# Token statistics summed in the state space, and an MLP that walks row block by row block

## The chip, the cores and the metric

The kernel runs on one core of one Trainium2 chip. The metric is the device time of one execution in microseconds; for the kernel before it is the median of three runs. The engines are named as in the profile: PE (TensorE), DVE (VectorE), ACT (ScalarE), POOL (GpSimd) and SP, which here only issues DMAs.

## The reference

Two transformer layers on 2048 tokens of width 512, batch 1, float32. Layer 0 is an attention and a mixture of eight experts; layer 1 is a selective state space and a block-diagonal MLP on permuted features. The change touches the last two parts:

```python
h = _layernorm(x, axis=-1) * (1 + ca) + sa
x = x + ga * _L1_attn_ref(h, ...)                  # state space
h = _layernorm(x, axis=-1) * (1 + cb) + sb
x = x + gb * _L1_ffn_ref(h, up, down, perm)        # MLP
# _layernorm: (x - mean) / sqrt(var + 1e-5), over the 512 features of a token
# _L1_ffn_ref: t = t[:, perm] in 16 heads of 32; gelu(t @ up) @ down per head; t[:, unperm]
```

The layer norm in front of the MLP needs the mean and the variance of each token over all 512 features of x behind the state space. The permutation moves features, so these sums don't depend on it.

## The kernel before

The stages run one after the other, each a block of five instruction streams, with a barrier of all engines between blocks. x lies feature-major: 512 features are four blocks of 128 partitions (`KT` = 4), and tokens run along the free axis.

**State space** (`state_space`, L1399 to L2157). 2048 tokens go in eight chunks (`SCH`) of 256 (`SW`). A chunk has 32 units or slots (`UNITS`): eight feature tiles t of the 1024 inner features, four state groups gr each, q = 4t + gr. Each engine walks over the slots in the order written out by hand in tables (`AT` for PE, `U_COPY`, `CONV_OUT`, `SILU`, `STEP_OUT`, `OUT_COPY` and others for ACT, `DELTA` and `GATE_Y` for DVE). In a slot ACT computes the decays (L2004) into one and a half units' worth of PSUM banks, DVE or POOL spreads the input, DVE scans (L2107), POOL multiplies by the read-out (L1689), and PE sums over states two slots later (`sum_states`, L1818) and adds the skip term (L1823). DVE multiplies the sum by the gate (`gate_y`, L2115). PE's sum of the next tile but one waits for that, since `ps_y` holds two tiles, one in each of PSUM banks 0 and 1. Projections, the convolution, step sizes and gates of the next chunk and the output projection of the chunk before (L1782) lie in slots in between. ACT copies the outputs (slots 14, 16, 20, 21) into `xout`, and SP stores them to the DRAM tensor `x_after_ssm` (L1605); for the last chunk this happens behind the loop, from two PSUM banks (L2068). SP's list per tile t: at t = 1 it loads the normalised rows of a later chunk and the residual `xres`, at t = 5 it stores, and for every tile it stores the step sizes and loads them back replicated (`repeat`, L1584 to L1594).

**MLP** (`permuted_mlp`, L2160 to L2327). Behind the barrier POOL gathers x from `x_after_ssm` by the permutation, one indirect DMA per block of 128 rows and all 2048 tokens (1 MB, L2205); blocks 0 and 1 count on one semaphore, 2 and 3 on another. SP loads the weights `up` and `down` (L2199, L2200), PE makes the bias (L2224) and ACT copies it. Then the norm, over four token chunks of 512: PE sums the mean over the four blocks (L2231), four rows at partitions 0, 32, 64, 96 of one bank; ACT copies it (L2286); PE spreads each row over 128 partitions by a matmul with ones (`spread`, L2236); DVE subtracts, one op of 128x2048 per token chunk (L2315); ACT squares (L2289); PE sums the variance (L2246); ACT takes Ln and Exp for 1/sqrt (L2293, L2295); PE spreads it, and DVE multiplies (L2320). The MLP proper is a loop over 16 quads, all four row blocks of token chunk 0 first, then those of token chunk 1 and so on. A quad is four heads in the 32-row strips of one row block, by 512 tokens: four up matmuls (L2265), four Gelus on ACT (L2303), four down matmuls (L2276), one DVE op that scales and adds x (L2326), and an indirect DMA of POOL to the output (L2213). Up results rotate over six PSUM banks.

## Time and profile before

| | us |
|---|---|
| median of 3 runs | 1711.09 (1709.91 to 1711.41) |
| the profiled execution | 1708.31 |
| its span | 1706.5 |
| DVE, PE, ACT, POOL busy in the span | 1322.2, 1436.1, 1132.7, 927.7 |

The span runs from the first to the last recorded instruction; the profiled execution's time has 1.8 us around it. The state space takes about 850 us of the span, up to the barrier at 1618; the MLP is the last 88 us. The shares of busy time are averages over stages with different limits and say little about either. Times in the rows are from the span's start. In a timeline a row is: start, length, engine, line, operation, out<-in, count, and in brackets the idle time before it and what ended it; PE rows count two records per float32 matmul. In the windows a row is: stretch, length, busy us and instructions of PE, PEld, DVE, ACT and POOL in this order, granted clock of TensorE as a share of 2.4 GHz, DMA share, GB/s. In groups by line it is: busy us, mean ns of one, idle time before.

### The profile page before, as it was taken

The page shows a single profiled execution, that of the slowest core. Times are in us where ns is not written, and L with a number is a line of the kernel's source. Part 1 is how long each engine was busy: PE and PEld are TensorE (multiplying, and loading weights), DVE is VectorE, ACT ScalarE, POOL GpSimd, SP SyncE. Part 2 cuts the span into 40 slices and gives each one's busy share as a digit, 9 for nine tenths or more (in the row PEclk, how much of TensorE's full clock was granted, in tenths as well). Part 3 has the DMA queues.
Part 4 walks back from the last instruction along what each step waited for, and adds up shares of the span by engine and source line. Part 5 has one row for each costly group of instructions (what it writes and reads, how often), then busy time and mean ns, then how long its engine had stood idle before and what let it go on. Part 6 is the DMA issues. An engine that isn't in the chain of part 4 may idle for free. (4 is left out here: it accounts for less than half of the span.)

```text
span 1706.5 us, 26217 instructions
## 1 busy us (share of the span) xinstructions
PE 1436.1 (84%) x8892; PEld 776.1 (45%) x8892; DVE 1322.2 (77%) x2119; ACT 1132.7 (66%) x2284; POOL 927.7 (54%) x602
## 2 busy tenths in 40 slices
PE   5888999999976895867798898988999989937768
PEld 2541222222224342645466565665656656614422
DVE  2329999999508413538999999999999999999742
ACT  3323677777854233558787978879788797875347
POOL 0000000000010223367999999999999999999703
PEclk8875899999996897779799999999999999958869
DMA  6411112222018345944454545555454554554222
GB/s 257 167 36 44 35 29 78 78 78 84 4 40 306 103 135 190 311 94 99 106 130 114 139 119 126 129 119 130 118 136 120 129 119 112 131 123 112 69 99 99
DMA packets 153865, 198.28 MB, mean 116 GB/s; under 512 B 17744, under 2 KB 124408, under 8 KB 152196
## 3 DMA queue, kind: packets, MB, share of 16 engines
q1 hardware_dynamic: 141443, 162.88, 35.4%
q0 software_dynamic: 5168, 18.63, 3.3%
q10 hardware_dynamic: 7120, 15.09, 2.4%
q8 instruction: 71, 1.16, 0.3%
q14 instruction: 63, 0.51, 0.1%
HBM read 150.68 MB, written 45.82 MB: 115 GB/s over the span
## 5 line engine op out<-in xcount | busy, mean ns | idle before, releaser
L2107 DVE TENSOR_TENSOR_SCAN shared<-ssm_psum,ssm_state,shared 128x256 f32<-128x256 f32 x1024 | 677.5, 737 | 21.0 <-ACT ssm_state L1991 12.3
L2004 ACT ACTIVATE ssm_psum<-shared,ssm_a 128x256 f32<-128x256 f32 x1024 | 444.5, 469 | 156.3 <-DVE shared L2107 146.2
L1689 POOL TENSOR_TENSOR shared<-shared,ssm_bc 128x1024 f32<-128x1024 f32 x256 | 509.2, 1999 | 33.3 <-DVE shared L2107 14.4
L735 ACT ACTIVATE att_probs<-att_psum 128x1024 f32<-128x1024 f32 x256 | 248.4, 1021 | 75.4 <-PE att_psum L662 72.9
L1666 POOL TENSOR_TENSOR shared<-shared,ssm_bc 128x1024 f32<-128x1024 f32 x144 | 287.7, 1998 | 10.2 <-DMA shared<-drive_rows 10.2
L776 DVE TENSOR_REDUCE att_rowmax<-att_psum 128x1 f32<-128x512 f32 x448 | 277.8, 683 | 3.4 <-PE att_psum L635 1.9
L1818 PE MATMUL ssm_psum<-shared,ssm_select 128*32 128x256 f32 x2048 | 167.3, 417 | 80.8 <-POOL shared L1689 80.2
L604 POOL COPY att_v<-v_tokens 128x128 f32<-128x128 f32 x8 | 2.3, 295 | 299.1 <-ACT att_out L729 299.1
L635 PE MATMUL att_psum<-att_k,att_q 32*128 32x512 bf16 x448 | 138.1, 398 | 10.0 <-DVE att_rowmax L776 7.3
L2092 DVE TENSOR_TENSOR shared<-shared,ssm_psum 128x1024 f32<-128x1024 f32 x112 | 135.0, 1205 | 8.6 <-DMA shared<-drive_rows 8.6
L674 PE MATMUL att_psum<-att_probs,att_v 128*32 128x512 f32 x1024 | 137.5, 609 | 0.6 <-ACT att_probs L735 0.6
L662 PE MATMUL att_psum<-att_q,att_k 32*128 32x512 bf16 (+2 forms) x1344 | 136.3, 385 | 0.0
L1730 PE MATMUL ssm_psum<-ssm_h,late_weights 128*128 128x256 f32 x448 | 117.1, 423 | 8.4 <-ACT shared L1964 8.1
L1818 PEld LDWEIGHTS ssm_psum<-shared,ssm_select 128*32 128x32 f32 x2048 | 46.7, 112 | 162.3 <-POOL shared L1689 82.8
L1782 PE MATMUL ssm_psum<-shared,late_weights 128*128 128x256 f32 x448 | 106.1, 391 | 6.4 <-ACT ssm_xout L1977 6.4
L1730 PEld LDWEIGHTS ssm_psum<-ssm_h,late_weights 128*128 128x128 f32 x448 | 93.8, 214 | 34.1 <-issue 9.3
L1774 PE MATMUL ssm_psum<-ssm_h,late_weights 128*128 128x256 f32 x448 | 105.4, 389 | 0.0
L1737 PE MATMUL ssm_psum<-ssm_upre,late_weights 128*128 128x256 f32 x448 | 102.9, 382 | 0.1
L662 PEld LDWEIGHTS att_psum<-att_q,att_k 18*128 18x128 bf16 (+2 forms) x1344 | 47.0, 93 | 114.9 <-ACT att_probs L735 89.7
L1782 PEld LDWEIGHTS ssm_psum<-shared,late_weights 128*128 128x128 f32 x448 | 85.6, 195 | 26.3 <-ACT ssm_xout L1977 8.8
L1774 PEld LDWEIGHTS ssm_psum<-ssm_h,late_weights 128*128 128x128 f32 x448 | 84.9, 193 | 19.3 <-issue 7.8
L1737 PEld LDWEIGHTS ssm_psum<-ssm_upre,late_weights 128*128 128x128 f32 x448 | 83.5, 189 | 17.5 <-issue 5.4
(274 smaller groups left out, 1845.5 us busy)
## 6 DMA issues: line engine op xcount, KB each, us to landing
shared<-drive_rows SPq DMA_DIRECT2D x256, 256.0 KB, 4.4
qkv_wmod<-in_wmod SPq DMA_DIRECT2D x8, 1536.0 KB, 12.2
shared<-in_x SPq DMA_DIRECT2D x8, 1024.0 KB, 5.0
...
ssm_bc<-bc_rows SPq DMA_DIRECT2D x32, 256.0 KB
...
sorted_results<-moe_y ACTq DMA_DIRECT2D x23, 256.0 KB, 2.0
```

Source lines behind the costliest of these rows:

```text
L662: last = nc.tensor.matmul(ps_s[half][:, j, :], kst[rows, s, a // 2, kt * P:(kt + 1) * P], qst[rows, s, a, :], start=(a == 0), stop=(a == P ...
L735: nc.scalar.activation(probs[:, u % RING, :].rearrange("p (j t) -> p j t", j=2), ps_s[u % 2], ACT.Exp).then_inc(exp_done, 1)
L776: nc.vector.tensor_reduce(rowmax[:, at:at + 1], ps_m[n % MB], AX.X, ALU.max).then_inc(max_done, 1)
L1666: nc.gpsimd.tensor_tensor(drive(Q), rep[:, s % 2, 1], bc[:, c % 2, 0, gr, :].unsqueeze(1).to_broadcast([P, J, SW]), ALU.mult).then_inc(poo ...
L1689: nc.gpsimd.tensor_tensor(read(Q), drive(Q), bc[:, c % 2, 1, gr, :].unsqueeze(1).to_broadcast([P, J, SW]), ALU.mult).then_inc(read_done, 1)
L1730: last = nc.tensor.matmul(halves("proj", c, pair)[:, i], win[:, k, m:m + P], rows_of(c)[:, k, :], start=(k == 0), stop=(k == KT - 1))
L1737: last = nc.tensor.matmul(halves("conv", c, pair)[:, i], conv[:, 2 * pair + i, k, :], upre[:, pair % 2, i, k:k + SW], start=(k == 0), stop ...
L1774: last = nc.tensor.matmul(halves("gate", c, pair)[:, i], win[:, k, m:m + P], rows_of(c)[:, k, :], start=(k == 0), stop=(k == KT - 1))
L1782: nc.tensor.matmul(bank("out", c, m)[:, 0:SW], wout[:, t, m * P:(m + 1) * P], gate[:, c % 2, t, :], start=(t == 0), stop=False)
L1818: last = nc.tensor.matmul(ps_y[t % 2][32 * j:32 * j + 32, :], select[:], read(Q)[:, j, :], start=(gr == 0), stop=False)
L2004: nc.scalar.activation(ps_decay[n % HALF_BANKS][:, i], rep[:, s % 2, 0, j, :], ACT.Exp, scale=amat[:, t, gr, j:j + 1]).then_inc(decay_done, 1)
L2107: nc.vector.tensor_tensor_scan(drive(Q)[:, j, :], ps_decay[(2 * Q + j // 2) % HALF_BANKS][:, j % 2], drive(Q)[:, j, :], state[:, t, gr, j: ...
```

## The change

In the state space, for each chunk c of 256 tokens: ACT squares the finished output `xout` (one Square of 128x1024, slot 22 of chunk c + 1) into a buffer that is free then (`xres`, for chunk 6 a part of `gate`); PE sums output and square over the features with `inv_d`, 32 equal rows each, into partitions 64 to 127 of the free half of PSUM bank 1 (slot 28, behind the sum of unit 26); ACT copies the 64 rows to SBUF (slot 31, in front of the Silu of the gate); SP stores one row of each kind to a new DRAM tensor `x_after_ssm_stats` at t = 1 of chunk c + 2. PE's first sum of tile 7 waits for that copy, as it writes the same bank. For the last chunk DVE makes the squares as products behind the loop, PE sums them last, and ACT copies them in the MLP straight from PSUM, which state space and MLP now share as one tensor (`g.tail_psum`).

In the MLP, SP first loads the rows back (four DMAs, each replicated over 32 partitions), then the weights. DVE makes the variance as mean square minus squared mean, not below zero; ACT takes Ln and Exp of all rows at once. PE spreads mean and 1/sqrt into all eight banks; DVE copies the means and ACT the 1/sqrt rows to SBUF, Gelu's table being loaded ahead of the latter. Each gather has its own semaphore. The quads now run row block by row block (q = 4k + i), and DVE centres and multiplies each quad's 128x512 by itself, three quads ahead (`AHEAD`) of the one whose output it adds. The mean, Square and variance work of the MLP is gone.

```diff
@@ state_space @@
+        ps_stat = psum[:, 1, SW:2 * SW]
+        def square_of(c):
+            return gate[:, c % 2, DT - KT:] if c == SCH - 2 else xres[:].rearrange("p s f -> p (s f)").rearrange("p (k t) -> p k t", k=KT)
...
+        SQUARE_OUT, STAT_MM, STAT_OUT = 22, 28, 31
...
+                if 1 <= c < SCH - 1:
+                    sp.wait_ge(stat_step, stat_ready(c - 1))
...
+            def store_stats(c):
+                sp.wait_ge(stat_step, stat_copied(c))
+                for n in range(2):
+                    sp.dma_start(scratch.stat[n:n + 1, c * SW:(c + 1) * SW], stat_rows[32 * n:32 * n + 1, :]).then_inc(stat_stored, 16)
...
+                    if t == 1 and c >= 2:
+                        store_stats(c - 2)
...
+                if (t, gr) == (DT - 1, 0) and c >= 1:
+                    pe.wait_ge(stat_step, stat_copied(c - 1))
...
+            def statistics(c):
+                pe.wait_ge(x3_done, (c + 1) * KT)
+                pe.wait_ge(stat_step, squared(c))
+                pe.wait_ge(ygate_done, (c + 1) * DT + DT - 2 if c < SCH - 1 else SCH * DT)
+                for k in range(KT):
+                    for n, rows in enumerate((xout, square_of(c))):
+                        last = nc.tensor.matmul(ps_stat[STAT_AT + 32 * n:STAT_AT + 32 * (n + 1), :], g.inv_d[:, 0:32], rows[:, k, :],
+                                                start=(k == 0), stop=(k == KT - 1))
+                last.then_inc(stat_step, 1)
...
+                    if c >= 1 and q == STAT_MM:
+                        statistics(c - 1)
...
+            def squares(c):
+                act.wait_ge(x3_done, (c + 1) * KT)
+                nc.scalar.activation(square_of(c), xout[:], ACT.Square).then_inc(stat_step, 1)
+            def copy_stats(c):
+                act.wait_ge(stat_step, stat_ready(c))
+                if c >= 1:
+                    act.wait_ge(stat_stored, 32 * c)
+                nc.scalar.copy(stat_rows, ps_stat[STAT_AT:, :]).then_inc(stat_step, 1)
...
+                    if c >= 1 and q == STAT_OUT:
+                        copy_stats(c - 1)
...
+                    if c >= 1 and q == SQUARE_OUT:
+                        squares(c - 1)
...
+            for b in range(MP // 2):
+                dve.wait_ge(out_mm, (SCH - 1) * KT + 2 * b + 2)
+                dve.wait_ge(stat_step, stat_copied(SCH - 2) + b)
+                rows = ps_m[b].rearrange("p (m s) -> p m s", m=2)
+                dve.wait_ge(x3_done, (SCH - 1) * KT + 2 * b + 2)
+                nc.vector.tensor_tensor(square_of(SCH - 1)[:, 2 * b:2 * b + 2, :], xout[:, 2 * b:2 * b + 2, :], rows, ALU.mult).then_inc(stat_step, 1)
...
@@ permuted_mlp @@
+            whole = T // W - 1
+            src = scratch.stat[:, 0:whole * W].rearrange("q (i t) -> i q t", i=whole)
+            for i in range(whole):
+                sp.dma_start(stat_rows[32 * i:32 * i + 32], src[i].unsqueeze(0).to_broadcast([32, 2, W])).then_inc(rows_in, 16)
+            sp.dma_start(stat_rows[32 * whole:, :, 0:SW], scratch.stat[:, whole * W:whole * W + SW].unsqueeze(0).to_broadcast([32, 2, SW])
+                         ).then_inc(rows_in, 16)
             sp.dma_start(up[:], d["up"].rearrange("p (k m) -> p k m", k=KT)).then_inc(weights_in, 16)
             sp.dma_start(down[:], d["down"].rearrange("p (h e) -> p h e", h=MH)).then_inc(weights_in, 16)
...
+            pe.wait_ge(rows_done, NCH + 1)
+            pe.wait_ge(rows_in, 16 * NCH)
+            pe.wait_ge(stat_step, 2)
+            for i in range(NCH):
+                spread(ps_mean, mean_rows, i).then_inc(spread_done, 1)
...
+            pe.wait_ge(bias_done, 2)
+            pe.wait_ge(stat_step, 7)
...
+                spread(ps_rstd, square_rows, i).then_inc(spread_done, 1)
...
-                    i, k = q // KT, q % KT
-                    pe.wait_ge(norm_done, i + 1)
+                    i, k = q % NCH, q // NCH
+                    pe.wait_ge(norm_done, 2 * q + 2)
...
@@ ScalarE @@
+            nc.scalar.copy(stat_rows[32 * (NCH - 1):, 0, SW:], ps_last[STAT_AT:STAT_AT + 32, :]).then_inc(stat_step, 1)
+            nc.scalar.copy(stat_rows[32 * (NCH - 1):, 1, SW:], ps_last[STAT_AT + 32:, :]).then_inc(stat_step, 1)
             nc.scalar.preload_act_table_set("natural_log_exp_and_others")
-            act.wait_ge(stat_mm, 1)
-            nc.scalar.copy(mean_rows[:], ps_stat).then_inc(mean_out, 1)
+            act.wait_ge(stat_step, 5)
+            nc.scalar.activation(square_rows, square_rows, ACT.Ln, bias=g.ln_eps[:, 0:1]).then_inc(stat_step, 1)
+            act.wait_ge(stat_step, 6)
+            nc.scalar.activation(square_rows, square_rows, ACT.Exp, scale=-0.5).then_inc(stat_step, 1)
+            act.wait_ge(bias_done, 1)
+            nc.scalar.copy(bias[:], ps_bias).then_inc(bias_done, 1)
+            nc.scalar.preload_act_table_set("gelu_and_others")
             for i in range(NCH):
-                act.wait_ge(centred_done, i + 1)
-                nc.scalar.activation(square[:, i], centred[:, :, i * W:(i + 1) * W], ACT.Square).then_inc(square_done, 1)
-            for pair in range(PAIRS):
-                r = slice(64 * pair, 64 * (pair + 1))
-                act.wait_ge(stat_mm, pair + 2)
-                nc.scalar.activation(rstd_rows[r, :], ps_var[pair][r, :], ACT.Ln, bias=g.ln_eps[r, 0:1]).then_inc(rstd_step, 1)
-                act.wait_ge(rstd_step, 2 * pair + 1)
-                nc.scalar.activation(rstd_rows[r, :], rstd_rows[r, :], ACT.Exp, scale=-0.5).then_inc(rstd_step, 1)
-            act.wait_ge(bias_out, 1)
+                act.wait_ge(spread_done, NCH + i + 1)
+                nc.scalar.copy(rstd_wide[:, i, :], ps_rstd[:, i, :]).then_inc(rstd_out, 1)
...
@@ VectorE @@
+            squared_mean = mean_wide[:, 0, :]
+            dve.wait_ge(rows_in, 16 * NCH)
+            dve.wait_ge(stat_step, 2)
+            nc.vector.tensor_tensor(squared_mean, mean_rows, mean_rows, ALU.mult).then_inc(stat_step, 1)
+            dve.wait_ge(stat_step, 3)
+            nc.vector.tensor_tensor(square_rows, square_rows, squared_mean, ALU.subtract).then_inc(stat_step, 1)
+            dve.wait_ge(stat_step, 4)
+            nc.vector.tensor_scalar(square_rows, square_rows, 0.0, None, ALU.max).then_inc(stat_step, 1)
             for i in range(NCH):
+                dve.wait_ge(spread_done, i + 1)
+                nc.vector.tensor_copy(mean_wide[:, i, :], ps_mean[:, i, :]).then_inc(mean_out, 1)
...
+            def normalise(q):
+                i, k = q % NCH, q // NCH
                 sl = slice(i * W, (i + 1) * W)
-                dve.wait_ge(spread_done, i + 1)
-                nc.vector.tensor_tensor(centred[:, :, sl], x[:, :, sl], ps_wide[i].unsqueeze(1).to_broadcast([P, KT, W]), ALU.subtract).then_inc(centred_done, 1)
-            for i in range(NCH):
-                sl = slice(i * W, (i + 1) * W)
-                dve.wait_ge(square_done, i + 1)
-                dve.wait_ge(spread_done, NCH + i + 1)
-                nc.vector.tensor_tensor(centred[:, :, sl], centred[:, :, sl], ps_wide[i].unsqueeze(1).to_broadcast([P, KT, W]), ALU.mult).then_inc(norm_done, 1)
+                dve.wait_ge(x_in[k], 16)
+                dve.wait_ge(mean_out, i + 1)
+                nc.vector.tensor_tensor(centred[:, k, sl], x[:, k, sl], mean_wide[:, i, :], ALU.subtract).then_inc(norm_done, 1)
+                dve.wait_ge(rstd_out, i + 1)
+                dve.wait_ge(norm_done, 2 * q + 1)
+                nc.vector.tensor_tensor(centred[:, k, sl], centred[:, k, sl], rstd_wide[:, i, :], ALU.mult).then_inc(norm_done, 1)
+            for q in range(AHEAD):
+                normalise(q)
             for q in range(QUADS):
-                i, k = q // KT, q % KT
-                if i >= 2:
-                    dve.wait_ge(g.out_stored[i % 2], i // 2 * 16 * KT)
+                i, k = q % NCH, q // NCH
+                if q + AHEAD < QUADS:
+                    normalise(q + AHEAD)
```

## Rows read from the trace of the kernel before

**Rows 1.** The chain of waits behind the barrier: start us, length us, what.

```profile
1618.19 0.06 issue
...
1622.83 10.95 DMA shared<-x_after_ssm,perm
...
1644.26 8.36 PE mlp_psum L2246 x32
```

**Rows 2.** The timeline, MLP stage, PE and ACT.

```profile
1622.31 1.88 PE L2224 MATMUL mlp_psum<-mod_permuted,mlp_up 32*128 32x1 f32 x32 [7.84 <-DMA mlp_down<-in_down]
...
1633.82 1.92 PE L2231 MATMUL mlp_psum<-shared,inv_d 128*32 128x512 f32 x16 [1.29 <-DMA shared<-x_after_ssm,perm]
...
1656.20 6.80 PE L2265 MATMUL mlp_psum<-mlp_centred,mlp_up_scaled 32*128 32x512 f32 x16 [1.02 <-DVE mlp_centred L2320]
...
1658.33 1.28 ACT L2303 ACT_TABLE_LOAD   x1 [4.32 <-PE mlp_psum L2265]
1659.62 4.74 ACT L2303 ACTIVATE mlp_hid<-mlp_psum,mlp_bias 128x512 f32<-128x512 f32 x8
...
1664.81 1.92 PE L2265 MATMUL mlp_psum<-mlp_centred,mlp_up_scaled 32*128 32x512 f32 x8
...
1666.76 32.52 ACT L2303 ACTIVATE mlp_hid<-mlp_psum,mlp_bias 128x512 f32<-128x512 f32 x56 [2.40 <-PE mlp_psum L2265]
```

**Rows 3.** A window of one chunk of the state space.

```profile
999.40:1105.00 105.60, 95.33 (x585) 66.05 (x584) 103.54 (x156) 87.44 (x214) 103.03 (x59) 0.95 0.52 125
```

**Rows 4.** The timeline, chunk 6, slots 28 to 31.

```profile
1494.00 1.07 PE L1818 MATMUL ssm_psum<-shared,ssm_select 128*32 128x256 f32 x16
...
1497.73 0.64 PE L1818 MATMUL ssm_psum<-shared,ssm_select 128*32 128x256 f32 x8 [2.03 <-POOL shared L1689]
...
1497.83 1.28 ACT L1968 ACT_TABLE_LOAD   x1
...
1499.98 1.08 PE L1818 MATMUL ssm_psum<-shared,ssm_select 128*32 128x256 f32 x8 [1.62 <-POOL shared L1689]
...
1503.35 2.68 DVE L2107 TENSOR_TENSOR_SCAN shared<-ssm_psum,ssm_state,shared 128x256 f32<-128x256 f32 x4 [0.89 <-ACT ssm_state L1991]
```

**Rows 5.** Groups by line and form, state space, ACT.

```profile
L1968 ACT ACTIVATE shared<-shared 128x2048 f32<-128x2048 f32 x7 | 13.4, 1912 | 0.1
...
L1926 ACT COPY ssm_proj<-ssm_psum 64x256 f32<-64x256 f32 x7 | 2.5, 355 | 0.0
```

**Rows 6.** The timeline, chunk 6, slots 22 and 23.

```profile
1471.37 2.67 DVE L2107 TENSOR_TENSOR_SCAN shared<-ssm_psum,ssm_state,shared 128x256 f32<-128x256 f32 x4
...
1472.21 0.58 ACT L1958 ACTIVATE ssm_psum<-ssm_psum 128x512 f32<-128x512 f32 x1
```

**Rows 7.** Waits of SP's queue, 900 to 1110: us in total, times, longest.

```profile
SPq L1584 <- POOL ssm_du L1653: 117.5, 16, 9.2
```

**Rows 8.** Groups by line and form, whole run, DVE.

```profile
L1365 DVE TENSOR_TENSOR shared<-shared 128x512 f32<-128x512 f32 x16 | 10.8, 676 | 9.6 <-DMA shared<-sorted_results,moe_result_int 9.6
...
L2315 DVE TENSOR_TENSOR mlp_centred<-shared,mlp_psum 128x2048 f32<-128x2048 f32 x4 | 8.9, 2282 | 18.7 <-PE mlp_psum L2236 18.7
...
L2326 DVE SCALAR_TENSOR_TENSOR mlp_y<-mlp_psum,mod_permuted,shared 128x512 f32<-128x512 f32 x16 | 12.0, 751 | 26.6 <-PE mlp_psum L2276 26.6
```

**Rows 9.** Windows around the barrier.

```profile
1614.00:1616.00 2.00, 0.47 (x3) 0.07 (x1) 0.00 (x0) 0.86 (x2) 0.00 (x0) 1.00 0.00 0
...
1626.00:1628.00 2.00, 0.00 (x0) 0.00 (x0) 0.00 (x0) 0.00 (x0) 0.00 (x0) 0.50 1.00 389
```

**Rows 10.** DMA issues, 1618 to 1640: count, KB, median us to landing.

```profile
mlp_up<-in_up SPq DMA_DIRECT2D x1, 256.0 KB, 2.6
mlp_down<-in_down SPq DMA_DIRECT2D x1, 256.0 KB, 3.5
```

**Rows 11.** The gathers' line, L2205, four of them.

```profile
DMA to landing us min/median/max: 7.4/9.1/10.9
```

**Rows 12.** Groups by line and form, 1611 to 1707, ACT.

```profile
L2293 ACT ACTIVATE mlp_rstd_rows<-mlp_psum,ln_eps 64x512 f32<-64x512 f32 x2 | 1.4, 684 | 2.7 <-PE mlp_psum L2246 2.7
```

## What was predicted

> **What bounds the kernel now.** I read the chain of waits first, then the timeline around it, then windows. The chain of waits [rows 1] covers only what follows the barrier in front of the MLP stage (1618.2 us); it shows which work ends last there. Up to 1656 us no Gelu can run: the gather of the last two row blocks, which share a semaphore, lands at 1633.8, and behind it stand one after the other the mean matmuls, the mean rows, the mean spread, two centrings, a Square, the 8.36 us of variance matmuls and the rstd spread. The first matmul of the MLP proper starts at 1656.20 and the first Gelu at 1659.62 [rows 2]. From there ScalarE sets the pace: 56 Gelus in 32.52 us, 0.58 each, 2.32 per quad of four [rows 2]. So 41 us (1618.3 to 1659.6) pass ahead of the first Gelu, and 46.9 us (1659.6 to the span's end at 1706.5) follow, which the change leaves alike in kind and number.
>
> Ahead of the barrier is the state space. In a whole chunk (105.6 us) VectorE is busy 103.5 us, ScalarE 87.4, POOL 103.0, PE 95.3 [rows 3]: VectorE is its bound, and of the 2 us that it idles per chunk 0.89 are a wait for ScalarE behind a Silu with its two table loads [rows 4].
>
> **Part 1: statistics inside the state space.** Per chunk but the last it adds a Square of 128x1024 on ScalarE (slot 22), eight matmuls of 32 columns' weights by 256 columns on PE (slot 28), a copy of 64x256 on ScalarE (slot 31), and two row stores of 1 KB on SP (a chunk later).
>
> Square: no row has this size; 128x2048 takes 1.91 us on that engine [rows 5], so about 1.0. It pushes what ScalarE does in slots 22 and 23, the step-size chain among it. In the trace that chain's Ln ends at 1472.79, and VectorE comes to use it after the scan of slot 22, at 1474.04 (1471.37 + 2.67) [rows 6]: 1.25 us of room, so cost 0. Uncovered it would be up to 1.0 in each of the six chunks with this chain (the last has no step sizes), 6 us.
>
> Copy: slot 31 runs into the Silu's table load, and VectorE waits 0.89 us at the end of this sequence [rows 4], so an op put here is paid in full. A 64x256 copy shows 0.355 us [rows 5]; ScalarE's starts lie closer than its durations, so I take 0.32, six times (the last chunk has no Silu behind it): +1.9 us. Bounds 0 and 0.45 x 6 = 2.7.
>
> Matmuls: the two 32-column groups run side by side if they behave as the four groups of the mean matmuls (16 records, two 128-row blocks of x, in 1.92 us at full clock: 0.96 per block for 512 columns) [rows 2]; for 256 columns 0.48 per block, four blocks 1.9 us. In slots 28 to 31 PE waits 2.03 us for POOL before the sum at 1497.73 [rows 4], which covers them. The new waits: PE's sum of unit 28 waits for ScalarE's copy (ready at 1498.2, 0.5 us after the sum would start; the sums of units 29 to 31 and the next chunk's projection are queued behind, and before the next sum PE waits another 1.62 us for POOL [rows 4], which swallows it). ScalarE's copy waits for the statistics (done by 1496.5 if they start behind the sum of 1494.00; ScalarE arrives at 1497.8 [rows 4]): no wait. Cost 0, at most 0.5 per chunk, 3.5.
>
> SP: the two stores stand in front of the loads at t = 1 of a chunk. SP waits 117.5 us for POOL's du in two chunks, 16 waits of up to 9.2 us [rows 7], so two issues of 0.4 us vanish there.
>
> End of the stage: VectorE's two products, 0.68 each [rows 8], follow ScalarE's two copies and end at about 1615.9; PE's eight matmuls then end at 1617.8 at full clock, and the clock in 1614 to 1616 is 1.00 [rows 9]. The barrier opens at 1618.2 for the store of x [rows 1], which is not touched. Cost 0; at the lower clock 1.5.
>
> **Part 2: the MLP's start.** It removes the mean and variance matmuls, the four 128x2048 Squares and the wait for all row blocks; each quad gets two 128x512 ops on VectorE. The new chain, in the old span's clock:
> 1. SP issues four row loads from 1618.37 at the weight loads' pitch of 0.4, ahead of the weights; the last starts at 1619.6. The nearest landings are 2.6 and 3.5 us for the two weight loads [rows 10], and 7.4 to 10.9 for the 1 MB gathers [rows 11]. I take 3.5: that load too was in flight with the first gather. Rows there at 1623.1. Bounds 2.6 and 9.1: 0.9 earlier to 5.6 later.
> 2. VectorE: three 128x512 ops, 0.68 each [rows 8], and 0.2 of hand-over: 1625.3. ScalarE: Ln 0.68 [rows 12], Exp taken alike, 0.1: 1626.8.
> 3. PE meanwhile: mean spreads, four row groups of 512 columns, taken as one block of the mean matmuls, 0.96 at full clock; the clock is at its lower level after this idle stretch (0.50 in 1626 to 1628 [rows 9]), so 1.9: 1625.1. Bias matmuls 1.88 [rows 2]: 1627.0 (the weights, issued up to 1.7 us later than before, land at 1623.9 by 3.5, under the spreads). Bias copy 0.2, rstd spreads 1.9: 1629.1. Gelu's table load, 1.28 and formerly in the chain [rows 2], runs beside them.
> 4. ScalarE copies the first rstd, 0.59: 1629.7. VectorE has copied the means by 1628.0 (4 x 0.68, no such row; nearest row, same width [rows 8]), the first row block has landed by 1626.4 (1619.02 + 7.4 [rows 11]) and is centred by 1628.7; the multiply, 0.68 and a hand-over, ends at 1630.5. Were that block the last to land, 1629.9, it would be 0.8 later.
> 5. From the first matmul to ScalarE's next action it takes 2.13 us (1656.20 to 1658.33 [rows 2]): first Gelu at 1632.6 for 1659.6. Gain 27.0 us.
>
> The loop behind: per quad VectorE does 0.68 + 0.68 + 0.75 = 2.11 us [rows 8], under ScalarE's 2.32, three quads ahead, so ScalarE still sets it. I keep the 46.9 us, with the cold start in it: before, up and down matmuls ran at the lower clock until about 1666, and the 2.40 us pause of Gelu comes from that [rows 2]. Without a cold stretch it would be 2.4 less.
>
> Here a rule speaks against the change. The rows show 0.676 us for 512 columns and 2.28 for 2048 [rows 8]: eight large ops become 32 small ones, 0.42 more per 2048 columns, 3.4 us in all, beside ScalarE. The Trainium skill, "VectorE: DVE Perf Modes", section "The TRN2 errata — SBUF-src ops pay a fixed extra latency per instruction", says that many small tiles pay that latency once each; by its formula (N+151)/0.96 the loss would be an estimated 3.8 us of engine time. The trace agrees, and shows where it would lie: under ScalarE's 2.32.
>
> **Sum.** 1706.5 - 27.0 + 1.9 = 1681.4 us of span, 25.1 less. The profiled execution took 1708.31, 1.8 around its span, so its like would take 1683.2; the median of the runs, 1711.09, is 2.8 above it. From the median: 1686.0.
>
> **Rivals.**
> A. Row loads and weights land as late as the gathers (9.1 us), all four of which are queued on the same engines. Rows at 1628.7, weights 1629.5, mean spreads 1630.6, bias 1632.5, rstd spreads 1634.6, copy, multiply and first Gelu 1638.0: +5.4, 1691.4. Against it: the second weight load landed in 3.5 us beside the first gather. The Trainium skill, "DMA: Bandwidth & Descriptors", section "Queues, rings and completion order", has each DMA engine take turns between its queues, packet by packet; by that rule the small loads share and the nearer value holds, as the 3.5 us row bears out.
> B. The loop gets slower. PE stays at the lower clock two quads longer: there an up quad took 1.92 us of PE [rows 2], its down matmuls taken alike: 3.84, 1.52 above 2.32, so +3.0, 1689.0; or VectorE's hand-overs bring its quad to 2.6, 0.28 x 16 = +4.5, 1690.5.
> C. The Square is not covered: +6, 1692.0. The room was 1.25 for 1.0, so a small part of it can appear.
> D. Slower than before: ScalarE stands in slot 31 and waits for the statistics, with the Silu, slot 31's decays and so VectorE's scan queued behind. If the column groups don't overlap and PE is at its lower clock, eight matmuls take 8 x 0.96 = 7.7 us (0.96 for 512 columns at full clock; doubled, halved for 256), to 1502.2; ScalarE, there at 1497.8, loses 4.4 and its 0.3, over six chunks 28: 1712 (1686.0 - 1.9 + 28). It decides from 4.5 us per chunk. Against it: PE's granted clock in a chunk is 0.95 [rows 3], and column groups overlap in the mean matmuls.
> E. The change doesn't do what it says: the first quad still awaits the last gather, 1633.8 + 0.68 + 0.68 + 2.1 = 1637.3, +4.7, 1690.7. Four separate semaphores speak against it.
>
> **Chances.** Forecast within 2.5 us: 0.45. A: 0.14. B: 0.15. C: 0.10. E: 0.02. Faster than that (no cold stretch, copy hidden, 1682): 0.10. D or another cost of its size: 0.04. Within 0.2% (3.4 us, about what a measurement of this kernel can tell from no change) only a half of D would land: 0.01 more or less. Faster 0.95, same 0.01, slower 0.04. The range takes in 1681 (loads at 2.6, no cold stretch, copy hidden: 0.9 + 2.4 + 1.9 less) and A or C with part of B: 1681 to 1695.
>
> **What would show it.** First Gelu 14 to 15 us behind the barrier, with no variance matmuls after the gathers; VectorE's wait behind slot 31 at 1.2 instead of 0.89 and a chunk of 105.9; no new wait behind slot 22; the weight loads issued at about 1620 and landed before 1625; Gelu at 2.32 us per quad without new gaps. The forecast is wrong if the row loads land after 1626, if ScalarE's queue shows waits for PE's statistics, or if Gelu's rate is worse than 0.58.

## The result, and the profile after

The ratio is 0.991, with a 95% interval from 0.9897 to 0.9923: 14.75 us faster. The forecast was 1686.0, within 1681 to 1695, 25.1 us faster. The sign was right and the size was not.

The two traces are compared by four marks, read from the timelines: VectorE's first multiply of the gate (s = 0), its last (s = 63), VectorE's first instruction in the MLP (the memset of `mlp_ones`, 0.3 us behind the barrier in the kernel before and 0.5 us in the changed one), and the first Gelu. The profiled span ends the last stretch. Each kernel that is told of below has its line; the median is over the timed runs.

| kernel | s = 0 to s = 63 | to the MLP's first | to first Gelu | to the end | median |
|---|---|---|---|---|---|
| before | 823.44 | 7.42 | 41.15 | 46.88 | 1711.24 |
| before, again | 823.17 | 7.42 | 40.58 | 46.95 | 1707.81 (1 run) |
| changed | 827.31 | 9.54 | 21.71 | 46.59 | 1696.49 |
| changed, again | 826.58 | 8.92 | 22.17 | 44.39 | 1696.66 |
| hold_all | 827.52 | 9.54 | 16.05 | 44.36 | 1690.09 |
| hold_rest | 827.56 | 9.53 | 18.62 | 46.45 | 1696.18 |
| weights_first | 827.73 | 9.53 | 24.66 | 46.88 | 1701.12 |
| weights_early | 827.35 | 9.56 | 17.92 | 46.75 | 1695.19 (1 run) |
| all_early | 827.50 | 9.56 | 11.75 | 46.45 | 1685.21 |
| late_copy | 825.54 | 9.56 | 20.92 | 46.95 | 1696.02 |
| thin_stats | 824.97 | 7.84 | 22.21 | 47.02 | 1695.32 |
| stat6_gap | 825.89 | 7.85 | 20.69 | 47.15 | 1694.12 |
| combo | 824.06 | 9.61 | 11.68 | 47.69 | 1682.17 |
| combo2 | 824.10 | 7.88 | 11.78 | 47.12 | 1683.66 |

The work ahead of s = 0 is not touched by the change; it ended between 787.1 and 793.9 us in these fourteen profiles and moves single profiles by as much as the change's smaller terms. With the means of the two profiles of each kernel, the changed one has +3.6 in the state space, +1.8 at its end, -18.9 ahead of the first Gelu and -1.4 behind it, together -14.9; the medians differ by 14.75. In the same four profiles the part ahead of s = 0 is 2.6 us longer in the changed kernel, so that their spans differ by 12.3 only. This shift is there long before the state space (VectorE's first instruction of the mixture of experts starts at 499.61 us before and at 501.05 in the changed kernel, first profiles) and no run explains it. That 14.9 comes so near to 14.75 is therefore in part chance.

The start of the MLP. First the chain of waits of the changed kernel behind the barrier (start us, length us, what), which answers to [rows 1]:

```profile
1630.22 11.82 DMA mlp_down<-in_down
...
1642.08 1.93 PE tail_psum L2308 x32
...
1644.26 2.13 PE tail_psum L2297 x8
1646.38 0.57 ACT mlp_rstd_wide L2357
...
1646.98 0.70 DVE mlp_centred L2393
```

The gathers are no longer in it, and neither are variance matmuls. In their place stands the second weight load, 11.82 us long. The timeline of the same stretch, answering to [rows 2]:

```profile
1627.73 1.25 SPq L2271 DMA_DIRECT2D mlp_stat_rows<-x_after_ssm_stats  x3
...
1628.38 1.01 POOL L2280 DMA_INDIRECT shared<-x_after_ssm,perm  x1 [11.08 <-POOLq L1429]
...
1629.03 0.43 SPq L2272 DMA_DIRECT2D mlp_stat_rows<-x_after_ssm_stats  x1
1629.50 0.68 SPq L2274 DMA_DIRECT2D mlp_up<-in_up  x1
1629.69 0.94 POOL L2280 DMA_INDIRECT shared<-x_after_ssm,perm  x1 [0.30 <-issue]
1630.22 0.43 SPq L2275 DMA_DIRECT2D mlp_down<-in_down  x1
...
1635.85 0.69 DVE L2375 TENSOR_TENSOR mlp_mean_wide<-mlp_stat_rows 128x512 f32<-128x512 f32 x1 [7.20 <-DMA mlp_stat_rows<-x_after_ssm_stats]
...
1638.52 0.63 ACT L2351 ACTIVATE mlp_stat_rows<-mlp_stat_rows 128x512 f32<-128x512 f32 x1
...
1642.08 1.88 PE L2308 MATMUL tail_psum<-mod_permuted,mlp_up 32*128 32x1 f32 x32 [4.07 <-DMA mlp_down<-in_down]
...
1649.91 1.27 ACT L2365 ACTIVATE mlp_hid<-tail_psum,mlp_bias 128x512 f32<-128x512 f32 x2 [1.49 <-PE tail_psum L2328]
```

The rows are there 8.1 us behind the barrier (1635.85 - 1627.73), the weights 14.4 (1642.08). The exponential is done at 1639.15 and 1/sqrt could be spread then; PE stands in front of the bias matmuls and waits for the weights until 1642.08. From there 7.8 us of work, in the order and nearly in the length of the forecast, lead to the first Gelu at 1649.91. The DMA view of 1626 to 1660 (KB each, median us to landing), answering to [rows 10], and of 1627 to 1644 (packets, MB and busy share by queue: q0 carries GpSimd's gathers, q1 SP's loads):

```profile
mlp_up<-in_up SPq DMA_DIRECT2D x1, 256.0 KB, 8.9
mlp_down<-in_down SPq DMA_DIRECT2D x1, 256.0 KB, 11.8
```

```profile
q0 software_dynamic: 576, 4.19, 63.2%
q1 hardware_dynamic: 608, 0.98, 18.3%
```

The loads took 8.9 and 11.8 us where the same two took 2.6 and 3.5 before, and gathers and loads together kept the DMA engines busy for four fifths of that stretch (63.2 and 18.3%).

The state space. VectorE's and ScalarE's timelines of the changed kernel: the wait behind slot 31 of chunk 6, which answers to the last row of [rows 4]; a multiply of the gate in chunk 5; a Square at slot 22.

```profile
1511.00 2.03 DVE L2170 TENSOR_TENSOR_SCAN shared<-tail_psum,ssm_state,shared 128x256 f32<-128x256 f32 x3 [1.28 <-ACT ssm_state L2049]
...
1389.86 0.42 DVE L2178 TENSOR_TENSOR shared<-tail_psum,shared 128x256 f32<-128x256 f32 x1 [0.86 <-PE tail_psum L1856]
...
1261.44 1.04 ACT L2029 ACTIVATE ssm_xres<-ssm_xout 128x1024 f32<-128x1024 f32 x1
```

Behind slot 31 VectorE waits 1.28 us where it waited 0.89, at six chunk ends. In chunks 4 and 5 it waits, once each, 0.89 and 0.86 us for PE at slot 27, where it did not wait before. No wait stands behind a Square.

### The profile page after: what moved, and what is told of

Its sections match the earlier page's. It is cut to its first block and busy times, and to the rows that moved or that the text cites. A ratio compares the mean times of both kernels' runs of the same rounds, so it can differ in the third digit from the quotient of the medians.

```text
span 1696.5 us, 26466 instructions
## 1 busy us (share of the span) xinstructions
PE 1421.8 (84%) x8956; PEld 772.0 (46%) x8956; DVE 1331.0 (78%) x2152; ACT 1133.1 (67%) x2297; POOL 929.7 (55%) x602
## 5 line engine op out<-in xcount | busy, mean ns | idle before, releaser
L2170 DVE TENSOR_TENSOR_SCAN shared<-tail_psum,ssm_state,shared 128x256 f32<-128x256 f32 x1024 | 675.6, 727 | 23.3 <-ACT ssm_state L2049 14.6
L2062 ACT ACTIVATE tail_psum<-shared,ssm_a 128x256 f32<-128x256 f32 x1024 | 443.0, 468 | 154.9 <-DVE shared L2170 144.5
L1851 PE MATMUL tail_psum<-shared,ssm_select 128*32 128x256 f32 x2048 | 170.0, 410 | 75.9 <-POOL shared L1720 70.6
L2155 DVE TENSOR_TENSOR shared<-shared,tail_psum 128x1024 f32<-128x1024 f32 x112 | 133.8, 1195 | 8.7 <-DMA shared<-drive_rows 8.7
L663 PE MATMUL att_psum<-att_q,att_k 18*128 18x512 bf16 (+2 forms) x1344 | 136.5, 385 | 0.0
L1761 PE MATMUL tail_psum<-ssm_h,late_weights 128*128 128x256 f32 x448 | 107.1, 396 | 8.6 <-ACT shared L2011 8.4
L1813 PE MATMUL tail_psum<-shared,late_weights 128*128 128x256 f32 x448 | 107.0, 393 | 7.6 <-ACT ssm_xout L2025 7.6
L1805 PE MATMUL tail_psum<-ssm_h,late_weights 128*128 128x256 f32 x448 | 108.7, 398 | 0.0
L1768 PE MATMUL tail_psum<-ssm_upre,late_weights 128*128 128x256 f32 x448 | 103.2, 382 | 6.2 <-ACT ssm_upre L1948 3.4
L1761 PEld LDWEIGHTS tail_psum<-ssm_h,late_weights 128*128 128x128 f32 x448 | 86.7, 198 | 29.8 <-ACT shared L2011 8.8
L1813 PEld LDWEIGHTS tail_psum<-shared,late_weights 128*128 128x128 f32 x448 | 86.1, 196 | 28.0 <-ACT ssm_xout L2025 10.1
L1805 PEld LDWEIGHTS tail_psum<-ssm_h,late_weights 128*128 128x128 f32 x448 | 87.2, 198 | 20.3 <-issue 7.8
```

The costliest lines, as they stand in the source:

```text
L663: last = nc.tensor.matmul(ps_s[half][:, j, :], kst[rows, s, a // 2, kt * P:(kt + 1) * P], qst[rows, s, a, :], start=(a == 0), stop=(a == P ...
L1761: last = nc.tensor.matmul(halves("proj", c, pair)[:, i], win[:, k, m:m + P], rows_of(c)[:, k, :], start=(k == 0), stop=(k == KT - 1))
L1768: last = nc.tensor.matmul(halves("conv", c, pair)[:, i], conv[:, 2 * pair + i, k, :], upre[:, pair % 2, i, k:k + SW], start=(k == 0), stop ...
L1805: last = nc.tensor.matmul(halves("gate", c, pair)[:, i], win[:, k, m:m + P], rows_of(c)[:, k, :], start=(k == 0), stop=(k == KT - 1))
L1813: nc.tensor.matmul(bank("out", c, m)[:, 0:SW], wout[:, t, m * P:(m + 1) * P], gate[:, c % 2, t, :], start=(t == 0), stop=False)
L1851: last = nc.tensor.matmul(ps_y[t % 2][32 * j:32 * j + 32, :], select[:], read(Q)[:, j, :], start=(gr == 0), stop=False)
```

## Why the loads are late: hold_all, hold_rest, weights_first, weights_early, all_early

Theory: the loads are issued behind the first gathers, share the DMA engines with them, and so land with them. Rival: the loads are slow by themselves, the row loads because one line of DRAM is repeated 32 times.

**hold_all** lets nothing run beside the loads.

```diff
+            pool.wait_ge(rows_in, 16 * NCH)
+            pool.wait_ge(weights_in, 32)
             for k in range(KT):
                 pool.indirect_dma_start(x[:, k, :], None, scratch.x3, bass.IndirectOffsetOnAxis(ap=g.perm[:, k:k + 1], axis=0)).then_inc(x_in[k], 16)
```

> The gathers of GpSimd wait until the row loads and both weight loads have landed, so that nothing runs beside these. Theory 1 (the loads land late because they share the DMA engines with four gathers): the rows land 4 to 5 us behind the barrier instead of 8.1, mlp_down 6 us behind it instead of 14.3, the first gather 13.5, and the first Gelu comes 16 us behind the barrier instead of 22.2; about 1690 us. Theory 2 (the loads are slow by themselves, the rows through the 32-fold repeat of one line and the weights behind them): landings stay at 8 and 14 us, the first gather lands at 22, the first Gelu comes 24.5 us behind the barrier; about 1699 us.

Measured: 1690.09 us (1689.26 to 1692.62), ratio to before 0.9862 (0.9831 to 0.9893). VectorE's timeline (the barrier is at 1629.92), ScalarE's, and landings in the DMA view:

```profile
1634.25 0.69 DVE L2377 TENSOR_TENSOR mlp_mean_wide<-mlp_stat_rows 128x512 f32<-128x512 f32 x1 [3.47 <-DMA mlp_stat_rows<-x_after_ssm_stats]
...
1646.44 37.20 ACT L2367 ACTIVATE mlp_hid<-tail_psum,mlp_bias 128x512 f32<-128x512 f32 x64 [1.49 <-PE tail_psum L2330]
```

```profile
mlp_up<-in_up SPq DMA_DIRECT2D x1, 256.0 KB, 3.1
mlp_down<-in_down SPq DMA_DIRECT2D x1, 256.0 KB, 3.1
```

The rows are there 4.3 us behind the barrier, the weights land in 3.1, and the first Gelu comes 16.05 us behind the MLP's first instruction, though the first gather is issued 5.6 us later than in the changed kernel (6.3 against 0.65 us behind the barrier). The theory stands; the repeat of one line is not what was slow.

**hold_rest** holds back gathers 1 to 3 alone (`if k == 1:` ahead of the same two waits, inside the loop).

> Only gathers 1 to 3 wait until the row and weight loads have landed; gather 0 is issued at once. Theory 1 (the four queued gathers hold the loads back): rows land some 5 us behind the barrier, mlp_down some 7.5, the first Gelu comes 14 to 16 us behind the barrier, and the later gathers land just ahead of their quads; 1688 to 1691 us. Theory 2 (the loads are slow by themselves): landings at 8 and 14 us as in the changed kernel, first Gelu at 22, and gather 1, which then lands 21 to 22 us behind the barrier, is in time; 1696 us.

Measured: 1696.18 us (1691.65 to 1698.26). VectorE's timeline (barrier at 1628.27), and a landing in the DMA view:

```profile
1636.04 0.69 DVE L2378 TENSOR_TENSOR mlp_mean_wide<-mlp_stat_rows 128x512 f32<-128x512 f32 x1 [6.86 <-DMA mlp_stat_rows<-x_after_ssm_stats]
```

```profile
mlp_down<-in_down SPq DMA_DIRECT2D x1, 256.0 KB, 7.2
```

The stretch to the first Gelu is 18.62 us, 3.3 less than in the mean of the changed kernel's two profiles, and not the 14 to 16 of the expectation: the rows are there at 7.8 us, hardly earlier than beside four gathers (8.1), the weights at 9.6 instead of 14.4. One gather in front is enough to make the rows late. The weights land 5.6 us behind the barrier without a gather (hold_all), 9.6 beside one and 14.4 beside four. In the medians this gain does not show (1696.18 against 1696.66 for the changed kernel in the same session, both ranges 6 us wide); only the stage shows it.

**weights_first** puts SP's two weight loads ahead of its four row loads.

> SP issues the two weight loads ahead of the four row loads. Theory 1 (a load that is issued before the gathers fill the DMA engines lands soon, one that is issued behind them lands late): mlp_down lands 5 to 8 us behind the barrier instead of 14.3, the rows 11 to 13 instead of 8.1, and the chain of the statistics, which takes 9 us from the rows to the first Gelu, ends at 20 to 22 us; 1694 to 1697 us. Theory 2 (each load needs its time, whatever runs beside it): weights 5, rows 10, first Gelu 19 us behind the barrier; 1693 us.

Measured: 1701.12 us (1699.04 to 1704.13), 4.5 slower than the changed kernel beside it. The timelines of GpSimd and VectorE (barrier at 1630.19):

```profile
1635.63 1.42 POOL L2283 TENSOR_SCALAR mlp_up_scaled<-mlp_up,mod_permuted 128x128 f32<-128x128 f32 x4
...
1645.73 0.69 DVE L2375 TENSOR_TENSOR mlp_mean_wide<-mlp_stat_rows 128x512 f32<-128x512 f32 x1 [14.62 <-DMA mlp_stat_rows<-x_after_ssm_stats]
```

The weights, issued ahead of the first gather as they were before the change, are there as soon as GpSimd is free (5.4 us behind the barrier); the rows, now issued behind it, need 15.5 us. The load that stands behind the gathers is the late one, whichever it is. That is worse than either expectation, for behind the rows the longer chain is still to come.

**weights_early** and **all_early** issue loads in the last chunk of the state space, into columns of the late weights that are free by then: the first the two weight loads, the second the row loads too (what follows `store_stats` in the diff is in all_early alone). The large buffers of the MLP then lie in memory of earlier stages too.

```diff
             load_residual(SCH - 1)
+            sp.wait_ge(conv_done, (SCH - 1) * DP)
+            sp.dma_start(g.up, d["up"].rearrange("p (k m) -> p k m", k=KT)).then_inc(g.mlp_in, 16)
+            sp.dma_start(g.down, d["down"].rearrange("p (h e) -> p h e", h=MH)).then_inc(g.mlp_in, 16)
             store_stats(SCH - 2)
+            sp.wait_ge(stat_stored, 32 * (SCH - 1))
...
+            for i in range(whole):
+                sp.dma_start(g.stat_rows[32 * i:32 * i + 32], src[i].unsqueeze(0).to_broadcast([32, 2, W])).then_inc(g.rows_in, 16)
...
             store(SCH - 1)
```

> Only the two weight loads are issued in the last chunk of the state space; the four row loads stay behind the barrier, beside the gathers. It tells what of the late start is the rows' and what the weights'. Theory 1 (both are held back by the gathers, the weights last): the rows land 8 us behind the barrier as in the changed kernel, the logarithm and exponential end 3.3 us behind that, and the first Gelu comes 17 to 19.5 us behind the barrier instead of 22. Theory 2 (only the rows matter): 22 us.

> The weight loads and the row loads are issued by SP in the last chunk of the state space, ahead of its last store, into columns of the late weights that are free by then; nothing is loaded beside the gathers. Theory 1 (the start of the MLP is bound by these loads): the first gather lands 8.4 us behind the barrier (1.0 to issue, 7.3 to land), its first centring, multiply and up matmuls follow, and the first Gelu comes 11 to 12 us behind the barrier instead of 22; 1685 to 1687 us. Theory 2 (something else of the start, such as the spreads of the statistics at half clock, ends nearly as late): 15 us or more behind the barrier, 1690 us. The loop behind the first Gelu takes 46.6 us as before; if gathers 1 to 3 land late for their quads, longer.

Measured: weights_early 1695.19 us in its one run, the stretch to the first Gelu 17.92 us: the weights' part of the delay is some 4 us. all_early 1685.21 us (1683.21 to 1689.78), ratio 0.9853 (0.9833 to 0.9873), the stretch 11.75 us. From VectorE's, ScalarE's and PE's timelines of all_early:

```profile
1631.86 0.73 DVE L2395 TENSOR_TENSOR late_weights<-shared,mlp_mean_wide 128x512 f32<-128x512 f32 x1 [1.09 <-DMA shared<-x_after_ssm,perm]
...
1631.97 0.17 ACT L2358 COPY mlp_bias<-tail_psum 128x16 f32<-128x16 f32 x1 [2.17 <-remote]
...
1632.19 2.09 PE L2302 MATMUL tail_psum<-late_weights,mlp_ones 1*128 1x512 f32 x8 [3.65 <-ACT mlp_bias L2358]
...
1637.85 4.73 ACT L2370 ACTIVATE late_weights<-tail_psum,mlp_bias 128x512 f32<-128x512 f32 x8 [1.49 <-PE tail_psum L2333]
```

VectorE now waits 1.09 us for the first gather, which in the forecast for the change landed in time. A new wait of 2.17 us stands ahead of ScalarE's bias copy, and the spreads of 1/sqrt wait for that copy (1632.19); the profile names no engine for the 2.17 us, and their cause stays open.

## What the statistics cost the state space: both kernels again, late_copy, thin_stats, stat6_gap

> The kernel before once more, unchanged, for a second profile of it. Five profiles of the changed kernel and its variants have 826.6 to 827.7 us from the first multiply of the gate (s = 0) to the last (s = 63), and 8.9 to 9.5 us from the last to the end of the stage, against 823.4 and 7.4 in the one profile of before. If these are costs of the change: 823 to 824 and 7.4 again, no DVE wait at slot 27, and 0.9 us behind slot 31. If they are chance: somewhere between the two. The start of the state space, 787.6 in the first profile of before and 789.3 to 793.4 in those of the changed kernels, should be anywhere in that span if it has nothing to do with the change.

> The changed kernel once more, unchanged, for a second profile of it. Where the first profile of the changed kernel stands above the one of before in stages that the change does not touch, a run to run difference would come out otherwise here, and a cost of the change would come back. Expected of the ends of stages: the last multiply of the gate (s = 63) at about 1607 us if its 3.7 us ahead of the state space were chance, 1611 if not. The DVE wait behind slot 31 comes back at 1.28 us in chunks 1 to 6 (a cost of the copy); the two DVE waits of 0.9 us in chunks 4 and 5 at slot 27, where the granted clock had dipped, and the tail's output matmuls of 5.3 us are chance and need not come back. First Gelu 22.2 us behind the barrier again. Time 1694 to 1698 us.

The kernel before came out as in its first profile, within 0.3 us in the state space and with the same 7.42 at its end; the changed one again lost 3.1 us there (one wait of 0.85 us at slot 27, this time in chunk 1) and 1.5 at the end. These are costs of the change; which chunks have a wait at slot 27, and how many, varies: two waits in hold_all, hold_rest, weights_first, weights_early, all_early and late_copy, one in stat6_gap, none in combo and combo2. My expectation that the output matmuls of 5.3 us were chance was wrong: they took 4.7 here, and 5.3 to 5.4 in eight other profiles, against 3.62 in the kernel before. The other 0.4 us that the end loses lie between the store of x and the MLP's first instruction (3.30 us before, 3.73 in the changed kernel and in thin_stats); no run asks why. The 1607 and 1611 us of the second expectation for s = 63 fit no mark of the changed kernel (1618.66, then 1615.92) and decide nothing.

**late_copy** moves ScalarE's copy of chunks 0 to 5 away from slot 31.

```diff
-        SQUARE_OUT, STAT_MM, STAT_OUT = 22, 28, 31
+        SQUARE_OUT, STAT_MM, STAT_OUT = 22, 28, 6
...
-                    if c >= 1 and q == STAT_OUT:
-                        copy_stats(c - 1)
+                    if c >= 2 and q == STAT_OUT:
+                        copy_stats(c - 2)
+                    if c == SCH - 1 and q == UNITS - 1:
+                        copy_stats(c - 1)
```

> ScalarE's copy of the statistics of chunks 0 to 5 is moved from slot 31, where it stands ahead of the last decays of a chunk, to slot 6 of the chunk behind it; the copy of chunk 6 stays. Theory 1 (the copy lengthens what VectorE waits for behind slot 31): the wait goes from 1.28 back to 0.9 us in the six chunk ends, the state space is 2.2 us shorter than in the changed kernel, 1694 us. Theory 2 (the 0.4 us come from the statistics matmuls or the Square, the copy is hidden): the waits stay at 1.28, no change of time. The two waits of 0.9 us at slot 27 and the tail, both with the clock of TensorE low, should not change by this.

```profile
1510.82 2.03 DVE L2176 TENSOR_TENSOR_SCAN shared<-tail_psum,ssm_state,shared 128x256 f32<-128x256 f32 x3 [0.88 <-ACT ssm_state L2053]
```

The wait behind slot 31 (VectorE's timeline, chunk 6) is back at 0.88 us, in all six chunk ends; the copy was the cost, 0.4 us each. The state space is 1.8 us shorter than in the first profile of the changed kernel, where 2.2 were expected: the two waits at slot 27 remain, and the wait ahead of the last multiply of the gate is 4.40 us instead of 3.44, as the last sums run at the lower clock here (granted 0.50 from 1616 to 1622). The median, 1696.02 (1688.22 to 1698.66), can't show that.

**thin_stats** leaves out three of the four row blocks of the statistics matmuls in chunks 0 to 6 (`for k in range(1)` there).

> In chunks 0 to 6 the statistics are summed from one of the four row blocks alone (this kernel leaves out three quarters of these sums), so that TensorE has 4 instead of 16 matmuls at slot 28; Square, copy and stores stay. Theory 1 (the added matmuls move the moment at which the clock of TensorE falls, to slots 24 to 27 in some chunks and onto the last output matmuls in the tail): the waits of 0.9 us at slot 27 go, the tail from the last multiply of the gate to the end of the stage takes 7.4 us instead of 9.5, and 1692 to 1693 us result. Theory 2 (these dips are chance, or come from the Square or the copy): one or two such waits and a tail of 9.5 remain, 1696 us.

Measured: 1695.32 us (1694.7 to 1697.43), state space 824.97, end 7.84. State space and end together are 4.0 and 2.7 us shorter than in the two profiles of the changed kernel; the median did not come down to the expected 1692 to 1693. All waits at slot 27 are gone, those of 1.27 us behind slot 31 are all there, as they should be. What ties the lost time to the clock are the windows. Chunk 5, the changed kernel and then thin_stats, whose chunks start 1 us apart (columns: window, length, busy time of PE, PEld, DVE, ACT, POOL, granted clock, DMA share, GB/s):

```profile
1382.00:1386.00 4.00, 3.81 (x11) 2.88 (x12) 4.00 (x7) 3.87 (x11) 4.00 (x3) 0.65 0.94 184
1386.00:1390.00 4.00, 4.00 (x26) 2.56 (x27) 3.14 (x6) 3.97 (x10) 4.00 (x4) 0.92 0.53 135
1398.00:1402.00 4.00, 2.40 (x23) 0.81 (x20) 4.00 (x6) 3.95 (x6) 3.66 (x4) 1.00 0.51 98
1402.00:1406.00 4.00, 4.00 (x19) 3.54 (x20) 2.73 (x6) 3.97 (x8) 2.62 (x2) 1.00 0.22 72
```

```profile
1382.00:1386.00 4.00, 4.00 (x22) 3.07 (x24) 4.00 (x6) 3.82 (x9) 4.00 (x3) 1.00 0.34 92
1386.00:1390.00 4.00, 3.68 (x32) 1.62 (x31) 4.00 (x8) 3.47 (x10) 4.00 (x4) 1.00 1.09 218
1398.00:1402.00 4.00, 2.95 (x19) 1.62 (x13) 3.78 (x6) 3.97 (x3) 3.81 (x3) 0.52 0.19 66
1402.00:1406.00 4.00, 4.00 (x13) 3.25 (x13) 2.94 (x5) 3.99 (x12) 2.19 (x2) 0.63 0.24 78
```

In thin_stats the clock is at its lower level (1.2 of 2.4 GHz) for most of 1398 to 1404, behind a quiet stretch of PE around slot 30, where no engine waits for PE; so it is in the kernel before (granted 0.50 from 1394 to 1400). In the changed kernel the statistics fill that quiet stretch (from 1394 to 1400 PE is busy for 5.45 us, in thin_stats for 2.79), the clock stays up there, and it falls within 1382 to 1387 instead, just ahead of the multiply at slot 27 (1389.86, above), which does wait for PE. The mean granted clock over the whole run is higher than before (0.899 against 0.883), and still VectorE lost time to it. The new place is not fixed: in the second profile of the changed kernel the clock stays at 1.00 from 1374 to 1412, and combo and combo2 run all statistics without a wait at slot 27. The end of the stage shows the same. PE's timelines of the output matmuls of the last two parts, in the changed kernel, in the kernel before (second profile) and in thin_stats:

```profile
1610.70 1.99 PE L1829 MATMUL tail_psum<-shared,late_weights 128*128 128x256 f32 x8
1618.46 5.30 PE L1829 MATMUL tail_psum<-shared,late_weights 128*128 128x256 f32 x16
```

```profile
1603.53 3.78 PE L1798 MATMUL ssm_psum<-shared,late_weights 128*128 128x256 f32 x8
1610.85 3.62 PE L1798 MATMUL ssm_psum<-shared,late_weights 128*128 128x256 f32 x16
```

```profile
1609.19 3.78 PE L1829 MATMUL tail_psum<-shared,late_weights 128*128 128x256 f32 x8
1616.53 3.62 PE L1829 MATMUL tail_psum<-shared,late_weights 128*128 128x256 f32 x16
```

and the windows, of the kernel before (second profile) and of the changed one:

```profile
1601.00:1605.00 4.00, 2.49 (x12) 1.44 (x13) 4.00 (x8) 1.88 (x5) 3.53 (x3) 0.60 0.00 0
1605.00:1609.00 4.00, 3.96 (x22) 1.92 (x20) 2.62 (x5) 0.00 (x0) 3.10 (x2) 0.55 0.00 0
1611.00:1615.00 4.00, 3.47 (x17) 2.71 (x15) 0.42 (x1) 1.02 (x2) 0.00 (x0) 1.00 0.00 0
```

```profile
1604.00:1608.00 4.00, 3.50 (x35) 1.65 (x34) 4.00 (x8) 2.37 (x6) 4.00 (x4) 1.00 0.00 0
...
1618.50:1621.50 3.00, 3.00 (x9) 2.44 (x8) 0.42 (x1) 0.00 (x0) 0.00 (x0) 0.54 0.00 0
```

Before, the clock fell at about 1602 on eight output matmuls (3.78 us) that nothing waited for, and was up again for the last sixteen (3.62), which end the stage. In the changed kernel, whose marks lie 7.6 us later, the statistics of chunk 6 keep PE busy ahead of that place (1604 to 1608, clock 1.00), the eight matmuls run at the upper level (1.99 us), and the clock falls at 1618.5, on the last sixteen: 5.30 us, 1.7 more, all on the path. In its second profile the clock falls on both (the last sixteen take 4.72 us). With a quarter of the statistics the old order is back.

**stat6_gap** keeps all the work and moves the statistics of chunk 6 from slot 28 into PE's wait ahead of the last state sums; the MLP copies their result from PSUM.

```diff
-                    if c >= 1 and q == STAT_MM:
+                    if 1 <= c < SCH - 1 and q == STAT_MM:
                         statistics(c - 1)
...
             for q in range(UNITS - LAG, UNITS):
+                if q == UNITS - 1:
+                    statistics(SCH - 2)
                 sum_states(SCH - 1, q)
```

> The statistics matmuls of chunk 6 are moved from slot 28 of the last chunk into the wait of 2.3 us that TensorE has ahead of the last state sums; their result stays in PSUM until the MLP copies it, so chunk 7 has no copy of statistics and the MLP one row load less. Theory 1 (16 busy matmuls at slot 28 push the fall of the clock onto the last output matmuls): from the last multiply of the gate to the end of the stage 7.4 to 7.9 us instead of 9.5, output matmuls 3.6 instead of 5.3 us; 1694 us. Theory 2 (the clock falls there whatever slot 28 does, or the moved matmuls push it there again): 9.5 us, 1696 us. The rest of the state space, with one or two waits at slot 27, is not changed by this.

```profile
1615.91 3.62 PE L1828 MATMUL tail_psum<-shared,late_weights 128*128 128x256 f32 x16
```

Measured: 1694.12 us (1692.06 to 1695.1), ratio 0.9893 (0.9878 to 0.9909); the end of the stage takes 7.85 us and its matmuls (PE's timeline) 3.62. The whole work can be there without the loss; its place decides. The MLP has one row load less in this kernel, so its later stretches are not compared.

## Both kernels beaten: combo and combo2

combo is late_copy and all_early together, combo2 adds stat6_gap.

> All loads early and the copies of chunks 0 to 5 at slot 6, together. If the two gains are independent: waits of 0.9 us behind slot 31, first Gelu 12.2 us behind the barrier, 2.2 us less than with the loads early alone: 1683 us. If the copy's place moves the clock of TensorE to a worse place again: 1685 to 1686 us.

> All three together: loads early, copies of chunks 0 to 5 at slot 6, statistics of chunk 6 in TensorE's wait ahead of the last state sums. If the gains add: state space 825 us, 7.4 to 7.9 us from the last multiply of the gate to the end of the stage, first Gelu 12.2 us behind the barrier, 1681 us, about 15 us less than the changed kernel. If the tail's clock falls on the output matmuls all the same: 1683 us.

Measured: combo 1682.17 us (1679.9 to 1686.25), ratio to before 0.9829 (0.981 to 0.9847); combo2 1683.66 us (1679.89 to 1686.39), ratio 0.9831 (0.9815 to 0.9847). Both beat the kernel before, in the same session, by 28 to 30 us; the changed kernel's median is 13 to 14 us above theirs. ScalarE's, PE's and VectorE's timelines of combo:

```profile
1632.41 4.73 ACT L2376 ACTIVATE late_weights<-tail_psum,mlp_bias 128x512 f32<-128x512 f32 x8 [1.49 <-PE tail_psum L2339]
```

```profile
1610.88 5.38 PE L1839 MATMUL tail_psum<-shared,late_weights 128*128 128x256 f32 x16
...
1611.12 0.42 DVE L2194 TENSOR_TENSOR shared<-tail_psum,shared 128x256 f32<-128x256 f32 x1 [4.40 <-PE tail_psum L1868]
```

Early loads and late copies add up (11.68 us to the first Gelu, 0.6 us lost in the state space). That so little is lost is not the copies' doing alone: no wait at slot 27 came in combo or combo2, and only the wait ahead of the last multiply of the gate is longer (4.40 and 4.24 us against 3.44). Of the third part, combo2's shorter end (7.88 against 9.61) is seen in the stage; in the medians it does not appear, the 1681 us of its expectation were not reached, and whether combo2 is faster than combo stays open.

121 lines of the change are left out of this document (58 added, 63 removed).

## The prediction, point by point

**The MLP's start: the path was right, two landings were mis-sized.** 27.0 us were to be gained, 18.9 were (mean of two profiles). The step that failed is the landing of the weights in step 3, and with it the ground on which rival A was set aside. Steps 2, 4 and 5 came out nearly as worked out: from rows to the end of the exponential 3.3 us (3.7 forecast), from the weights' landing to the first Gelu 7.8 (the forecast's pieces make 7.4). The two landings:
- Step 1, the row loads: 3.5 us taken, 6.8 measured behind the last issue; the rows were there 8.1 us behind the barrier instead of 4.9, within the bounds given.
- Step 3, the weights: "issued up to 1.7 us later than before, land at 1623.9 by 3.5", 5.7 us behind the barrier; measured 14.4. In the sum this term had no bound of its own, and it ended last.

The fault lies in how [rows 10] were read. The timeline of the kernel before, SP's and GpSimd's queue:

```profile
1618.77 0.43 SPq L2200 DMA_DIRECT2D mlp_down<-in_down  x1
1619.02 1.02 POOL L2205 DMA_INDIRECT shared<-x_after_ssm,perm  x1 [9.33 <-POOLq L1428]
```

The 3.5 us load had been issued 0.25 us ahead of the first gather, and the forecast put it down as "in flight with the first gather". In the changed kernel the four row loads come first, and the two weight loads are issued behind the first and the second gather. hold_all (3.1 us) and weights_first (the rows late in the weights' place) show that it is this order that decides.

Rival A had the mechanism, with 9.1 us for the landings and 1691.4 us in all. The weights took longer still (11.8), the rows less (6.8); by its own path A comes to 19.8 us ahead of the first Gelu (1618.2 to 1638.0), and 22.2 were measured (1627.73 to 1649.91). What was said against A, and the use made there of the Trainium skill, "DMA: Bandwidth & Descriptors", section "Queues, rings and completion order", fell with it. Its rule, that a DMA engine takes turns between its queues packet by packet, is not contradicted: in the changed kernel the loads' 608 packets carry 0.98 MB and the gathers' 576 carry 4.19 MB, so if these packets are what takes turns, the loads get about a fifth of the bytes and end about when the gathers do. The last load landed at 1642.0, and the slowest gather 12.1 us behind its issue, at 1644.3 if it was the one issued last (1632.18). The conclusion that the nearer value holds because loads "share" took bytes for packets. No run varied the size of the packets, so this reading is argued, not shown.

**Copy: right.** +1.9 us forecast, 0.32 each; VectorE's wait grew by 0.39 (0.89 to 1.28) in six chunks, 2.3 us, within the 2.7 of the bound. late_copy shows that it was the copy.

**Square, SP's stores, new waits: right.** No wait stands behind the Square (1.04 us for the 1.0 taken). C and D did not come: no wait of ScalarE for the statistics shows.

**Statistics matmuls and end of the stage: wrong.** Both were costed at 0, since PE had room (2.03 us of wait [rows 4]). The room was there. But filling it moved the moment at which the clock falls: one or two waits of 0.85 to 0.89 us at slot 27, and 1.7 and 1.1 us on the last output matmuls in the two profiles. The sum looked for waits of one engine on another and left out that the clock would fall elsewhere. The forecast had a bound of 1.5 "at the lower clock" for the end of the stage, on the statistics of the last chunk; those ran at full clock and were covered, and the loss fell on the matmuls ahead of them, which the change does not touch. The other 0.4 us at the end were not foreseen and are not explained.

**The loop: right.** 46.59 us against 46.88 before; Gelu at 2.32 us per quad with VectorE beside it, so B did not come. The cold stretch behind the first Gelu, priced at 2.4 us, is there in most kernels and missing in the second profile of the changed kernel and in hold_all, whose loops take 44.4 us; hold_all's 64 Gelus run in one piece of 37.20 us.

In sum, 25.1 us were forecast: 8.1 less at the start, some 0.4 more for the copies, some 1.3 for the waits at slot 27 and 1.8 at the end, against 1.4 gained behind the first Gelu, leave 14.9; the medians differ by 14.75. The 1.4 are luck: they come almost wholly from the one profile of two without the cold stretch.

## What to carry to other kernels

A landing time is a time beside certain neighbours: before using one, look in the timeline at what was queued ahead of that DMA, and count what will be queued ahead of it after the change; small loads that open a chain belong in front of the big transfers, best in the stage before. Filling idle time of TensorE isn't free just because the time is idle: look where the granted clock falls now and which matmuls stand where it will fall then. And a term of the sum needs a bound of its own even where others seem to cover it; the one that had none was the largest miss.
